# Feed-forward kernel: softmax sums made by products with 64 columns of ones, on chip, and values products moved into the score banks

## What is computed

```python
qkv = shift_token(x) @ wqkv                     # 128 -> 3 * 512, 8 heads of 64
q, k = rotary_xpos(l2norm(q) * qs, l2norm(k) * ksc)
sim  = einsum('bhwid,bhwjd->bhwij', bq * 8, bk)  # window of 64 against itself and the one before
attn = softmax(where(mask, -max, sim), axis=-1)
out  = einsum('bhwij,bhwjd->bhwid', attn, bv)
x = x + out @ wo
h = layernorm(shift_token(x)) @ w1 + b1
a, g = split(h, 2)
x = x + (a * gelu(g)) @ w2 + b2
```

## Time and profile before

| | |
|---|---|
| median of 3 runs | 2013.71 us |
| lowest and highest | 2003.6 and 2022.67 us |
| profiled execution, its own time | 2018.05 us |
| its span in the profile | 2016.3 us |
| TensorE matmuls busy | 1696.7 us (84%) |
| VectorE busy | 1337.8 us (66%) |
| ScalarE busy | 915.7 us (45%) |
| GpSimd busy | 800.3 us (40%) |
| granted TensorE clock, mean | 0.948 of full |

### The profile page before, as it was taken

One profiled execution on the slowest core, in us unless ns is written; L12 is line 12 of the kernel. 1 busy time (PEld: TensorE's weight loads), 2 busy tenths in 40 slices (PEclk: granted clock), 3 DMA queues, 4 the chain that ended last, 5 costly groups with the idle time before them and its releaser, 6 DMA issues. The chain is left out here.

```text
span 2016.3 us, 47867 instructions
## 1 busy us (share of the span) xinstructions
PE 1696.7 (84%) x19770; PEld 987.0 (49%) x19770; DVE 1337.8 (66%) x2021; ACT 915.7 (45%) x1455; POOL 800.3 (40%) x561
## 2 busy tenths in 40 slices
PE   3678888888898886799999994788888998888886
PEld 2345555555555554455555542445554555555543
DVE  4567776667776664577777754567777666667752
ACT  2234444455455443255555552344544554445442
POOL 3445445555554452100000003455555544555530
PEclk9689999999999998799999996889999999999998
DMA  4344454544444452322222201445444445554441
GB/s 145 40 72 73 67 82 74 79 83 67 73 77 67 80 77 59 105 84 74 87 93 79 85 11 14 62 73 83 70 67 73 77 68 82 78 89 84 73 88 32
DMA packets 82762, 148.55 MB, mean 74 GB/s; under 512 B 15039, under 2 KB 25715, under 8 KB 80371
## 3 DMA queue, kind: packets, MB, share of 16 engines
q1 hardware_dynamic: 81771, 142.81, 38.3%
q10 hardware_dynamic: 776, 2.68, 0.3%
HBM read 66.00 MB, written 16.52 MB: 41 GB/s over the span
## 5 line engine op out<-in xcount | busy, mean ns | idle before, releaser
L1095 POOL TENSOR_TENSOR QK<-QK,RB 128x1024 f32<-128x1024 f32 x128 | 302.9, 2368 | 447.7 <-DMA RB<-RN 447.3
L894 DVE SCALAR_TENSOR_TENSOR TP<-banks,cols,tab 128x1024 f32<-128x1024 f32 x256 | 321.1, 1276 | 117.3 <-PE banks L519 95.9
L1089 POOL TENSOR_TENSOR QK<-TP 128x512 f32<-128x512 f32 x128 | 165.0, 1289 | 253.8 <-DVE TP L894 194.1
L519 PE MATMUL banks<-rounded,wqkv_h 128*128 128x512 f32 x512 | 189.6, 453 | 72.4 <-POOL rounded L1081 45.9
L1391 ACT ACTIVATE PTL<-banks 128x1024 f32<-128x1024 f32 (+1 forms) x192 | 168.3, 884 | 168.8 <-PE banks L1311 168.8
L1462 DVE TENSOR_REDUCE NM<-banks 128x2 f32<-128x1024 f32 (+3 forms) x256 | 203.3, 820 | 54.6 <-PE banks L1280 54.1
L731 ACT ACTIVATE SQ<-banks 128x512 f32<-128x512 f32 x128 | 76.5, 597 | 293.2 <-PE banks L519 293.2
L917 DVE TRANSPOSE_TENSOR_REDUCE MX<-banks 128x16 f32<-128x512 f32 x256 | 160.3, 682 | 57.0 <-PE banks L556 57.0
L935 DVE TENSOR_TENSOR OT<-banks,OT 128x512 f32<-128x512 f32 x128 | 85.4, 688 | 149.1 <-DMA OT<-sums_d 136.4
L519 PEld LDWEIGHTS banks<-rounded,wqkv_h 128*128 128x128 f32 x512 | 97.8, 202 | 148.2 <-issue 73.6
L589 PEld LDWEIGHTS banks<-PT,V 128*64 128x64 f32 x4096 | 128.9, 139 | 74.4 <-issue 50.7
(11 more groups left out here) (179 smaller groups left out, 3033.5 us busy)
## 6 DMA issues: line engine op xcount, KB each, us to landing
RB<-RN SPq DMA_DIRECT2D x512, 64.0 KB, 4.0
OT<-sums_d SPq DMA_DIRECT2D x128, 256.0 KB, 4.0
V<-V SPq DMA_DIRECT2D x32, 512.0 KB, 6.0
V<-V SPq DMA_DIRECT2D x32, 384.0 KB, 7.0
rows_d<-SQ SPq DMA_DIRECT2D x48, 256.0 KB, 3.1
RB<-vars_d SPq DMA_DIRECT2D x32, 256.0 KB, 3.2
V<-rows_d SPq DMA_DIRECT2D x32, 256.0 KB, 2.7
RB<-rows_d SPq DMA_DIRECT2D x32, 256.0 KB, 3.0
```

The costliest lines, as they stand in the source:

```text
L519: last = nc.tensor.matmul(BK[4 + z][:, :], w[:, l, o:o + P].bitcast(F32R), h[:, :].bitcast(F32R), start=(k == 0), stop=(k == 2))
L894: nc.vector.scalar_tensor_tensor(out=TP[:, o:o + 2, :], in0=BK[4 + z][:, :].unsqueeze(1).to_broadcast([P, 2, T]), scalar=q, in1=tab[:, e, ...
L1089: nc.gpsimd.tensor_tensor(QK[:, m, 0, :], TP[:, 2, :], TP[:, 1, :], ALU.subtract)
L1095: nc.gpsimd.tensor_tensor(QK[:, m, :, :], QK[:, m, :, :], RB[:, m, :].unsqueeze(1).to_broadcast([P, 2, T]), ALU.mult).then_inc(S["nr_ok"], 1)
```

## The change

The softmax sums no longer leave the chip. For each chunk `j` of two heads, two products with 64 columns of ones put the two heads' sums on the 64 partitions each where `attended` needs them; ScalarE's Ln and Exp write the reciprocal straight into `OT[:, j, :]`. There are four such chunks a unit, where there were two halves. The stores and loads through `sums_d`, the tile `DR` and three semaphores are gone. All sums are now made beside the attends; none stand between the scores and projection 3. Banks change: the sums use 4, 7, 0 and 1, the values products 2, 3, 7 and 5 (before 6, 7, 6, 4). `hidden(1, 0)` moves behind the join and `hidden(1, 1)` behind projection 0, and on ScalarE the two gates follow. On VectorE `back` moves ahead of the first `attended`. The attention preparation uses banks 2, 3 and 2 in place of 0, 1 and 2. What each element of the result is computed from does not change.

```diff
-        ones32 = sb("ones32", [P, 32])
+        ones64 = sb("ones64", [P, W])
...
                     @block.sync
-                        def sums(u, g):
-                            n = 2 * u + g
-                            sp.wait_ge(S["dl_ok"], n + 1)
-                            sp.dma_start(sums_d[n % 2], DR[0:P:32, :]).then_inc(S["d_out"], 16)
-                            sp.wait_ge(S["d_out"], 16 * (n + 1))
...
-                                sp.dma_start(OT[W * e:W * e + W, 2 * g:2 * g + 2, :],
...
-                            run(sums, n - 2, 1)
                             run(norms, n - 1)
...
-                            run(sums, n - 1, 0)
...
                     @block.tensor
-                        def sums(u, g, k):
-                            pe.wait_ge(S["ex_ok"], 8 * u + 4 * g + 4)
-                            claim(k, "dn_ok", 2 * u + g + 1)
-                            for i in range(4):
-                                last = nc.tensor.matmul(BK[k][32 * i:32 * i + 32, :], ones32[:, :], PT[:, g, i, :],
+                        def sums(u, j, k):
+                            pe.wait_ge(S["ex_ok"], 8 * u + 4 * (j // 2) + 4)
+                            claim(k, "dn_ok", 4 * u + j + 1)
+                            for e in range(2):
+                                last = nc.tensor.matmul(BK[k][e * W:(e + 1) * W, :], ones64[:, :],
+                                                        PT[:, j // 2, 2 * (j % 2) + e, :],
...
                             run(attend, n - 2, 0, 6)
-                            run(sums, n - 2, 1, 4)
+                            run(sums, n - 2, 0, 4)
                             run(back, n - 4, 7)
                             run(tokens, n, 7)
...
-                            run(hidden, n - 3, 1, 0, 5)
-                            run(attend, n - 2, 1, 6)
+                            run(attend, n - 2, 1, 5)
+                            run(sums, n - 2, 1, 7)
                             run(attend, n - 2, 2, 4)
-                            run(values, n - 1, 0, 6)
-                            run(attend, n - 2, 3, 5)
-                            run(values, n - 1, 1, 7)
-                            run(values, n - 1, 2, 6)
-                            run(values, n - 1, 3, 4)
+                            run(sums, n - 2, 2, 0)
+                            run(values, n - 1, 0, 2)
+                            run(values, n - 1, 1, 3)
+                            run(attend, n - 2, 3, 6)
+                            run(sums, n - 2, 3, 1)
+                            run(values, n - 1, 2, 7)
+                            run(values, n - 1, 3, 5)
...
                             run(join, n - 2, 7)
-                            run(hidden, n - 3, 1, 1, 6)
+                            run(hidden, n - 3, 1, 0, 6)
                             run(project, n, 0)
+                            run(hidden, n - 3, 1, 1, 7)
                             run(scores, n - 1, 0)
...
                             run(scores, n - 1, 1)
-                            run(sums, n - 1, 0, 7)
                             run(project, n, 3)
...
                     @block.scalar
+                        def sums(u, j, k):
+                            act.wait_ge(S["dd_in"], 4 * u + j + 1)
+                            if u >= 1 and j == 0:
+                                act.wait_ge(S["wo_in"], u)
+                            nc.scalar.activation(OT[:, j, :], BK[k][:, :], ACT.Ln).then_inc(S["dn_ok"], 1)
+                            act.wait_ge(S["dn_ok"], 4 * u + j + 1)
+                            nc.scalar.activation(OT[:, j, :], OT[:, j, :], ACT.Exp, scale=-1.0).then_inc(S["dl_ok"], 1)
...
                     @block.vector
-                            dve.wait_ge(S[("d0_in", "d1_in")[j // 2]], 32 * (u + 1))
+                            dve.wait_ge(S["dl_ok"], 4 * u + j + 1)
...
+                            run(back, n - 3, 7)
                             run(attended, n - 1, 0, 6)
                             run(norms, n)
-                            run(attended, n - 1, 1, 6)
-                            run(back, n - 3, 7)
+                            run(attended, n - 1, 1, 5)
```

53 lines of the change are left out of this document (20 added, 33 removed).

## The result

The changed kernel takes 2003.47 us (median of 20 runs, 1998.63 to 2012.17). The kernel before, run beside it, takes 2014.11 us (20 runs). The ratio is 0.995, with a 95% interval of 0.9932 to 0.9968: half a per cent faster, so no change by the measure of one per cent. The profiled execution of the changed kernel took 2006.91 us (span 2005.1), 11.1 less than the one of before.

The account below looks back on a forecast made before the run. GpSimd's norm arm was taken to bound the unit. Steady +3.6, early units -7, drains -7.8 and first units +2 gave -9.2, profiled 2018.05 to 2009; with the median 4.3 below the profiled run, 2004 us, range 1980 to 2034.

Parts of the forecast that it names:

- norm arm: Unit's path from norm products through RN, SyncE's copies and GpSimd's normalisation to the scores; claimed to set the unit.
- join arm: TensorE's join and GpSimd's low part behind it; join forecast to start at +14.0, before +13.5.
- The detour on ScalarE: First sums' Ln and Exp queued ahead of the norms': RN at +8.8 instead of +6.2, eating the 2.2 us queue gain.
- Pairs side by side: TensorE's two 64-column sums products per chunk run side by side, taken as 1.0 us a pair.
- Steady units, +0.2 each: Units 7 to 15 of each phase: GpSimd starts 0.2 us later; eighteen units, +3.6 us.
- Units 1 to 6, gain 0.6 each, 7 in all: Early units of each phase: scores at +21.3 instead of +21.9, of twelve units 7 us gained.
- The drains, 7.8: Ends of both phases: gains of 2.6 and 1.2 us, plus 4.0 from joins running less long.
- The first units, +2: First units of each phase, TensorE at half clock half the time, chunks of sums 1.93 us each: 2 us added.
- clock rival: Sums fill TensorE's waits, so a third of 72 half-clock us in phase two's first units runs full: 1989 us, chance 0.25.
- Pairs one after the other: Rival: TensorE's sums pairs take 1.8 us, costing 2.6 a unit, 78 in all: 2082 us, chance 0.08.
- The detour paid in full: Rival: norm copies land no sooner, +1.2 in each of 18 steady units, early ones even: 2028 us, chance 0.12.
- The removal doing all that it promises: Rival: RN at +6.2, 2.2 us in 18 units, 40 more; no own chance beyond a twentieth, inside the clock rival's.

Follow-up runs that it names:

- Values last: Changed kernel with all values products behind attend 3 and sums 3 on TensorE, their copies behind sums 3 on ScalarE: 2002.3 us, ratio 0.9941.
- norms first: Changed kernel with the norms' Ln and Exp ahead of the first sums' on ScalarE, norm steps ahead of the first attended product on VectorE: 2000.05 us, 0.9919.
- both: Changed kernel with the edits of "norms first" and "values last" together: 1961.92 us, ratio 0.9731 against the kernel before.
- the added traffic: Changed kernel with two 256 KB copies into a spare tile put ahead of the norm copies in SyncE's queue: 2033.89 us, ratio 1.0085.
- same issues, few bytes: The added-traffic kernel with its two copies cut to 8 elements a row: 2022.39 us, ratio 1.0036 against the kernel before.
- last bank: Changed kernel with hidden(1, 1) and its gate using bank 4 instead of 7 in each phase's last pass: 2005.18 us, ratio 0.9971.
- sums twice: Changed kernel with every pair of sum products made two times for the same result: 2101.39 us, ratio 1.0428 against the kernel before.
- the repeat: The changed kernel run again without an edit: 2005.02 us, ratio 0.9953 against the kernel before.

## Why the prediction was right, and where its sum was not

The time came out 0.5 us from the forecast 2004, and that closeness is luck. The mechanism of a unit was as forecast, and so was the gain of the early units. But the steady units were forecast to lose 3.6 us and gained 5.9, and the drains were forecast to gain 7.8 and lost 1.2 (0.9 gained with the attention phase, 2.1 lost at the end). These errors, 9.5 one way and 9.0 the other, cancelled.

**What bounds a steady unit: right.** Two arms, norm and join, end within a microsecond of each other. "Values last" shows that the norm arm sets the unit, "norms first" that the join is close behind, and "both" that only the two together pay. The join arm itself was taken too long: forecast at +14.0, half a microsecond later than before, it starts at 13.71 on average, from 13.83. In the unit shown, it takes 0.98 us from the start of an attend to that of its sums and 0.86 from there to the next attend, where I had 1.04 and 1.0.

**The detour on ScalarE: right.** `RN` was forecast at +8.8 and the first issue at +8.85; they came at +8.53 and +8.56. The sums' Ln started at +3.9 and some of the instructions start 0.1 us before the one ahead of them ends, which I had added up without.

**Pairs side by side: right.** I took 1.0 and measured 1.03, with 0.86 to the next start. For a block of two, the 64-column shape costs nearly what the four 32-column products did.

**Steady units, +0.2 each: wrong in sign.** They gained 0.4 in the scores and 0.37 in the period, 5.9 us in all instead of a loss of 3.6. The failing step is the sum of the norm arm, "GpSimd starts at +15.2", 0.2 later than before: it came at 14.81, 0.5 earlier than the 15.32 of before. These 0.7 us are three mis-sized terms. The issue came 0.3 earlier than forecast, as above. I read the arm before at one unit, at 15.03, and that unit was the shortest of its phase's steady ones, 0.3 below the average, nearly all of it in its landing (6.63 where the average is 6.87). And the landing after was 6.26, 0.1 under the 6.3 to 6.4 that I took. So the landing went down by 0.6 and not by 0.2 or 0.3; about half of that is shown by the added traffic.

**Units 1 to 6, gain 0.6 each, 7 in all: right in sum, for a partly different reason.** The stretches of units 0 to 6 gained 6.8 us. Units 3 to 6 gained 0.9 each, more than forecast, and units 0 to 2 of the two phases together lost 0.3. The join arm ends last there, as forecast (see "values last"). The issue fell from 9.58 to 8.81, forecast from 9.4 to 8.85, and "same issues, few bytes" shows this term by itself: with the issue put back to +10.23 the scores come at +22.55. Where I expected the join at +15.2 and the scores at +21.3, they came at 14.89 and 21.29. The three lines of the early unit that answer to the earlier trace rows are these:

```profile
286.97 1.92 PE L523 MATMUL banks<-SQ,cst 128*32 128x512 f32 x16
...
301.82 3.70 PE L584 MATMUL banks<-OT,wo_s 128*128 128x512 f32 x8 [0.74 <-DVE OT L923]
...
308.34 1.04 PE L531 MATMUL banks<-bandb,identb 128*128 128x512 bf16 x4
```

**The drains, 7.8: wrong in the sum.** Most of the local gains came. Here is TensorE of the changed kernel in drain one (the first attend and its sums, the join) and in drain two (the turned maxima, `outward`, the join):

```profile
781.03 1.98 PE L574 MATMUL banks<-PT,V 128*64 128x64 f32 x32
782.79 1.92 PE L562 MATMUL banks<-PT,ones 128*64 128x512 f32 x4
...
791.19 3.60 PE L584 MATMUL banks<-OT,wo_s 128*128 128x512 f32 x8
...
1947.91 0.30 PE L549 MATMUL banks<-cst,MX 128*64 128x128 f32 x1 [2.67 <-DVE MX L905]
1948.05 4.47 PE L617 MATMUL banks<-GL,w_s 114*128 114x512 f32 x6
...
1964.51 3.70 PE L584 MATMUL banks<-OT,wo_s 128*128 128x512 f32 x8 [2.15 <-DVE OT L923]
```

Both joins are short, 3.60 and 3.70 us where they took 5.40 and 6.75: 4.85 us, where I had taken 4.0. In drain two the join comes 10.29 us after the first attend (1964.51 less 1954.22) instead of 11.66, a gain of 1.4 where I had 1.2. In drain one, counted from the last unit's norm products, the join comes 0.8 us earlier (60.55 against 61.33) where I had 2.6; the first attend and its sums ran at the half level of the clock (granted 0.50 from 780 to 784.5), 3.5 us together instead of 1.8, which is nearly all that is missing. With the 1.8 us by which its join is shorter, drain one was 2.6 ahead; the last pass then took 1.7 more, for the reused bank 7 (see "last bank"), and 0.9 was left, which is what the whole stretch gained. The forecast saw `hidden(1, 1)` in bank 7 and looked only at its cover in a steady unit; what the bank does where nothing covers it was put at nothing.

In drain two the clock took the gain back. There `outward` before the attends took 4.47 us instead of 2.78 (granted clock 0.62 from 1948 to 1952.5, against 1.00 before), and the last pass ran its hidden products at the half level (0.69 from 1978 to 1994.5, against 0.88 before), with the 0.87 us for bank 7 among them. The same place before, and in the changed kernel run again, where `outward` is short:

```profile
1959.64 0.30 PE L565 MATMUL banks<-cst,MX 128*64 128x128 f32 x1 [1.67 <-DVE MX L917]
1959.78 2.78 PE L632 MATMUL banks<-GL,w_s 114*128 114x512 f32 x6
```

```profile
1944.08 0.30 PE L549 MATMUL banks<-cst,MX 128*64 128x128 f32 x1 [2.67 <-DVE MX L905]
1944.22 2.78 PE L617 MATMUL banks<-GL,w_s 114*128 114x512 f32 x6
```

Here a second term that I booked at nothing shows. Before, the 1.06 us of half-0 sums stood in TensorE's wait for the maxima; they are gone, and TensorE idles 2.67 us there instead of 1.67. Whether `outward` then falls to the half level differs from one execution to the next. I read it in eleven profiles of kernels that have this order (all but "sums twice"): in four it is short, the repeat among them, and in seven long (4.25 to 5.35 us). In drain one the same step was long in eight of the eleven and short (2.78) in the kernel before. The repeat took 92.20 us from the last unit's norm products to the end, the first profile 94.88, the kernel before 92.79 (one profile). So the drain's loss of 2.1 us is within what the same code does from one execution to the next; that the moved sums make the longer outcome more likely is not shown.

**The first units, +2.** By itself this term can't be told from the gains beside it: with two gains of 0.6 a phase it comes to a gain of 0.4 for units 0 to 2 of both phases, and they lost 0.3. The mean clock of the first units of phase two was 0.75, and the same stretch, now 1189 to 1334, has 0.79. That is 61 of 145 us at the half level instead of 72: a sixth less, where the *clock rival* wanted a third, and with no visible effect on the stretch of units 0 to 6, which gained as much in phase one. In the steady stretches the clock rose from 0.99 and 0.98 to 1.00, mostly because six stretched joins went. The joins of the whole program are 10.8 us shorter, before and then after:

```profile
L599 PE MATMUL banks<-OT,wo_s 128*128 128x512 f32 x256 | 129.1, 652 | 7.2 <-DVE OT L935 7.2
```

```profile
L584 PE MATMUL banks<-OT,wo_s 128*128 128x512 f32 x256 | 118.3, 605 | 24.9 <-DVE OT L923 24.9
```

Of that 4.85 us are the drains'. Of the other long joins of before, six stood in steady units (4.32 to 5.29 us each). In three of these the scores still waited 0.26 to 0.54 for GpSimd behind them, and in the other three TensorE came without a wait; their scores came at +20.7 to +21.7, hardly later than in the units beside them. So I read this part as bought for almost nothing; no run tested it.

**The other rivals.** Pairs one after the other: excluded by the 1.03 us, and priced by "sums twice". The detour paid in full (2028): its detour is there, but the norm copies did land sooner. The removal doing all that it promises (40 us) was excluded for the changed kernel, rightly; with ScalarE's order changed back and the values products moved, 44 us come. That is near the 40 by chance in part: "norms first" alone brought some 6, and the rest needed the join arm shortened too, which the rival did not have.

## What to carry to other kernels

When two arms of a unit end within a microsecond of each other, an edit that shortens one shows little, and so does an edit that shortens the other: measure them together before dropping either. When a transfer is replaced by work on an engine, look at what is queued behind that work on the same engine; here a wait for TensorE in front of the norms' logarithm gave back what the shorter DMA queue had won. And read a term that repeats eighteen times from the average of the units, not from one of them.

## What the runs showed of the hardware that was not expected

Two DMA issues on SyncE took 1.35 us of its queue with 8 elements a row and with 512, so two issues right ahead of an urgent copy counted for more (17 us) than their 512 KB (some 10 us); issued earlier, with their bytes, they cost 3. The same program ran a block of six products at 2.78 us in one execution (granted clock 1.00) and 4.47 in the other (0.62), after the same 2.67 us of idleness. TensorE stopped for 0.7 to 3.2 us inside the score products of single steady units for what the trace calls issue, in six of thirteen profiles (2.33 in "norms first"); no run shows the cause. Two products of 64 columns by 512 in 32-bit floats took 1.03 us, and four of 32 columns 1.06, so the wider shape costs a pair no more than the narrow one costs four.
